# Layer 1 of a four-layer kernel: the experts' output bias fetched block by block, token counts by a scan, state-space products on two halves of the partitions

## What is computed

```python
# mixer
delta = softplus(x_inner @ W_dt + b_dt)
mean_delta = delta.mean(axis=-1)
a = exp(A[None, None, :] * mean_delta[..., None])        # 64 decays per token
bx = x_inner @ W_xp + b_xp                               # 64 inputs per token
state = a_t * state + bx_t                               # over 1024 tokens
s_sum = state.sum(axis=-1)
out = (s_sum[..., None] * x_inner * silu(res)) @ W_out + b_out + x * D
# feed-forward
shared = relu(normed @ sw1 + sb1) @ sw2 + sb2
comb = zeros(T, E).at[tokens, idx].add(w)                # w: the two weights of a token
h = relu(einsum('td,edh->teh', flat, ew1) + eb1)
eo = einsum('teh,eho->teo', h, ew2) + eb2                # eb2: the output bias, one row per expert
routed = einsum('teo,te->to', eo, comb)
return shared + routed
```

## Time and profile before

| | |
|---|---|
| time, median of 3 runs | 689.71 us (682.87 to 690.74) |
| profiled execution, span | 695.2 us |
| TensorE busy | 626.4 us (90%) |
| VectorE busy | 412.0 us (59%) |
| ScalarE busy | 366.7 us (53%) |
| GpSimd busy | 242.3 us (35%) |
| chain that ended last: TensorE | 59% of the span |
| DMA, mean of the span | 64 GB/s |

### The profile page before, as it was taken

The page is one execution under the profiler, slowest core; times in us unless marked ns, Lnnn a source line. Parts: engine busy times, 40 slices in busy tenths (PEclk is TensorE's granted clock), DMA queues, the critical chain, the costliest instruction groups (busy, mean ns, idle before and its releaser), DMA issues.

```text
span 695.2 us, 12273 instructions
## 1 busy us (share of the span) xinstructions
PE 626.4 (90%) x4105; PEld 404.3 (58%) x4108; DVE 412.0 (59%) x894; ACT 366.7 (53%) x849; POOL 242.3 (35%) x226
## 2 busy tenths in 40 slices
PE   8999999988987999888988889898888988799796
PEld 2885337974856667656656544345566665645353
DVE  6868754733345434956666478645868386455644
ACT  6346936325663443577478444362458468554342
POOL 2000660262373002757456323032138235523031
PEclk9999999989998999999999999999999999999999
DMA  8900212553443310000000210130000000040120
GB/s 302 361 20 0 95 58 86 155 163 123 135 128 102 98 62 28 24 9 2 16 17 1 68 58 0 38 101 1 16 1 2 1 1 1 8 117 0 48 91 16
DMA packets 29725, 44.48 MB, mean 64 GB/s; under 512 B 3928, under 2 KB 16064, under 8 KB 29152
## 3 DMA queue, kind: packets, MB, share of 16 engines
q1 hardware_dynamic: 26688, 36.48, 16.6%
q0 software_dynamic: 2976, 7.21, 3.4%
HBM read 34.37 MB, written 9.31 MB: 63 GB/s over the span
## 4 chain that ended last, share of the span: by engine, by line
PE 59%; DVE 18%; ACT 9%; issue 9%; POOL 3%; another core or an unknown queue 1%; DMA 1%; DVEq 0%; ACTq 0%; SPq 0%; POOLq 0%
PE bank L573 55%; ACT arena L1201 7%; DVE arena L2262 2%; DVE arena L2247 2%; DVE arena L2305 2%; POOL arena L2582 1%; DVE arena L2256 1%; DVE arena L2406 1%; DVE arena L2270 1%; PE bank L1067 1%; DVE bank L2298 1%; ACT rs L1201 1%; POOL arena L2590 1%; PE bank L948 1%; PE bank L762 1%
## 5 line engine op out<-in xcount | busy, mean ns | idle before, releaser
L1201 ACT ACTIVATE arena<-bank 128x512 f32<-128x512 f32 (+9 forms) x224 | 125.6, 565 | 102.8 <-PE bank L573 53.7
L1201 ACT ACTIVATE arena<-bank,arena 128x128 f32<-128x128 f32 (+1 forms) x244 | 87.8, 387 | 124.3 <-PE bank L573 61.5
L573 PE MATMUL bank<-arena,w 128*64 128x128 f32 (+2 forms) x528 | 143.2, 418 | 5.1 <-ACT arena L1201 5.0
L573 PE MATMUL bank<-arena 64*128 64x256 f32 (+8 forms) x832 | 108.8, 328 | 6.1 <-ACT arena L1201 6.1
L573 PE MATMUL bank<-xn_b,w 128*128 128x512 f32 (+1 forms) x192 | 91.4, 598 | 7.0 <-DVE arena L2406 3.8
L573 PEld LDWEIGHTS bank<-arena 64*128 64x128 f32 (+3 forms) x832 | 73.2, 169 | 33.1 <-ACT arena L1201 17.7
L573 PE MATMUL bank<-arena,work 128*128 128x128 f32 x624 | 85.7, 284 | 6.7 <-DVE arena L2152 2.6
L573 PEld LDWEIGHTS bank<-arena,work 128*128 128x128 f32 x624 | 78.2, 196 | 20.1 <-issue 16.0
L573 PEld LDWEIGHTS bank<-arena,w 128*128 128x128 f32 (+1 forms) x528 | 61.4, 163 | 39.1 <-issue 29.0
L573 PEld LDWEIGHTS bank<-xn_b,w 128*128 128x128 f32 (+1 forms) x192 | 34.5, 189 | 45.6 <-issue 28.6
L2490 POOL DMA_INDIRECT slots_in<-arena x32 | 33.8, 1057 | 77.2 <-ACT arena L1201 67.9
(11 more groups left out here) (222 smaller groups left out, 905.6 us busy)
## 6 DMA issues: line engine op xcount, KB each, us to landing
work<-in_ew SPq DMA_DIRECT2D x46, 256.0 KB
w<-kept SPq DMA_DIRECT2D x32, 128.0 KB, 3.0
work<-kept SPq DMA_DIRECT2D x32, 128.0 KB, 3.1
slots_in<-work SPq DMA_DIRECT2D x2, 1472.0 KB, 17.7
arena<-slots_in SPq DMA_DIRECT2D x10, 256.0 KB
slots_out<-arena POOLq DMA_DIRECT2D x10, 256.0 KB
w_ew<-in_ew SPq DMA_DIRECT2D x1, 2048.0 KB, 11.9
w<-in_p SPq DMA_DIRECT2D x1, 1840.5 KB, 9.8
```

The costliest lines, as they stand in the source:

```text
L573: return nc.tensor.matmul(o, lhsT, rhs, start=start, stop=stop, skip_group_check=True)
L1201: return nc.scalar.activation(o, i, f, bias=bias, scale=scale, **kw)
```

## The change

Four things change in layer 1, and nothing elsewhere.

1. **Output bias.** `cmb1`, its transposes, their copies and the product with `eb2` go. SP reads a second offset per block (`block_d`) and fetches that expert's 128 bias values into `bias2`, broadcast to 128 partitions (64 KB of writes), by a second DMA beside the weights'. `evicted` becomes a tensor_tensor add of PSUM and `bias2` in place of the copy.
2. **Token counts.** `cnt` is laid out expert by chunk, VectorE makes the counts of the chunks before by one scan of 72 elements (`before`), and TensorE needs two products for what took nine.
3. **State-space products.** `bx`, "md", the decays and the scan hold tokens 0 to 255 of a group on partitions 0 to 63 and 256 to 511 on 64 to 127. Products of 64 x 512 become two of 64 x 256 on the two halves. ScalarE reads [128 x 256] where it read [64 x 512]. The scan becomes two in sequence, with the last state of the one copied over to the other half (`seam`).
4. The weights' set "first" has one DMA more (`w1s` twice) and a wider constant (72 columns); "one" has one DMA less.

```diff
-                    mm(o, causal, cnt[:], stop=False)
-                    for c in range(1, 2 * C + 1):
-                        i = mm(o[:, c:], K["ones"], cnt[:, 0:2 * C + 1 - c], start=False, stop=c == 2 * C)
-                    i.then_inc(*step("cnt_p"))
+                    mm(o, ones, before[:], stop=False)
+                    mm(o[:, :, 0:2 * C], causal, cnt[:, :, 1:], start=False).then_inc(*step("cnt_p"))
...
+                    v.tensor_tensor_scan(before[:].rearrange("p e c -> p (e c)"), later, cnt[:].rearrange("p e c -> p (e c)"),
+                                         0.0, ALU.mult, ALU.add).then_inc(*step("before"))
...
+                    d = nc.values_load(block_d[0:1, n, k % NBLK:k % NBLK + 1], engines=[mybir.EngineType.SP], min_val=0,
+                                       max_val=(E1 - 1) * D)
+                    q, m = group(k), k % NBLK % SB
+                    if m == 0 and q >= 3:
+                        sp.wait_ge(*at_of(0, "rows_out", q - 3))
+                    sp.dma_start(bias2[:, q % 3, m], eb2.rearrange("(a e) d -> a (e d)", a=1)[:, bass.ds(d, D)].to_broadcast([P, D])).then_inc(
+                        bias2_in[q % 3], 16)
...
-                    pe.wait_ge(*at("cbt_s", g))
-                    mm(o[:], w_eb2, cbt1[:, gs(g)], start=False).then_inc(*step("sh", g))
-
-                def combined():
-                    pe.wait_ge(*at("cmb1"))
...
-                        i = mm(o[0:ST], W1["wxp"][:, j * ST:(j + 1) * ST], xi[:, j, gs(g)], start=j == 0, stop=j == 1)
+                        for h in range(2):
+                            i = mm(o[half_of(h), 0:GT // 2], W1["wxp"][:, j * ST:(j + 1) * ST], xi[:, j, hs(2 * g + h)],
+                                   start=j == 0, stop=j == 1)
...
-                    mm(o[0:ST], mean[:, 0:ST], dab[:, g]).then_inc(*step("md", g))
-                    yield
-                    o = fresh("quick", "ss", g)
+                    for h in range(2):
+                        i = mm(o[half_of(h), 0:GT // 2], mean[:, 0:ST], dab[:, g, hs(h)])
+                    i.then_inc(*step("md", g))
+                    yield
+                    o = fresh_pair("ss", g)
                     pe.wait_ge(*at("states", g))
-                    mm(o[:], ones[:], states[:, gs(g)]).then_inc(*step("ss", g))
+                    for h in range(2):
+                        i = mm(o[h][:, 0:GT // 2], ones[half_of(h)], states[half_of(h), hs(g)])
+                    i.then_inc(*step("ss", g))
...
+                    for h in range(2):
+                        start = 0.0
+                        if g or h:
+                            last = (2 * g + h) // 2 * GT // 2 - 1 if h == 0 else (g + 1) * GT // 2 - 1
+                            after()
+                            v.tensor_copy(seam[half_of(h), g:g + 1], states[half_of(1 - h), last:last + 1]).then_inc(*step())
+                            after()
+                            start = seam[half_of(h), g:g + 1]
+                        v.tensor_tensor_scan(states[half_of(h), hs(g)], decay[half_of(h), hs(g)], bx[half_of(h), hs(g)],
+                                             start, ALU.mult, ALU.add).then_inc(*step(*(("states", g) if h else ())))
...
-                        v.tensor_copy(rows_out[:, q % 2, 0:n], psum("eo", q)[:, 0:n * P].rearrange(
-                            "p (b d) -> p b d", d=P)).then_inc(*step("rows_out", q))
+                        dve.wait_ge(bias2_in[q % 3], 16 * sum(len(blocks_of(i)) for i in range(q % 3, q + 1, 3)))
+                        v.tensor_tensor(rows_out[:, q % 2, 0:n], psum("eo", q)[:, 0:n * P].rearrange(
+                            "p (b d) -> p b d", d=P), bias2[:, q % 3, 0:n], ALU.add).then_inc(*step("rows_out", q))
```

110 lines of the change are left out of this document (51 added, 59 removed), and 2 rows, old and new, of the table BESIDE.

## The result

| | before | after |
|---|---|---|
| time, median of 20 runs each | 685.48 us (682.22 to 691.64) | 680.93 us (676.01 to 684.64) |
| ratio after / before | | 0.9925, 95% interval 0.9904 to 0.9945 |
| profiled execution, span | 695.2 us | 676.3 us |

What follows compares the result with a forecast made beforehand. TensorE, busy 90% of the span, was taken to bound the kernel; -1.2 + 2.5 - 6.5 + 1.0 + 0.2 = -4.0 us gave 685.7 us from the median 689.7 (profiled 691.2), range for 8 in 10 676 to 695.

Steps and rivals of the forecast that it cites:

- the first case: Main forecast, the sum of the terms: 685.7 us from the median, own range 682 to 689, chance 0.50.
- rival 1: The clock does not fall and the gather absorbs nothing: -9.1 us, 680.6 us, chance 0.17.
- Ahead of the first block: TensorE sheds 7.2 us there but waits for expert rows; only the counts' 1.2 us is kept.
- Clock: TensorE's new wait for the first rows drops its clock to 0.50: 2.5 us lost, bounds 0 and 3.
- Beside the blocks: TensorE sheds 9.1 us beside the expert blocks; 2.6 us count as absorbed by the gather, so 6.5 us remain.
- SP: Added bias fetches in SP's queue cost 1.0 us in all, from dense runs of blocks; room on average.
- The wider set at the start: The wider "first" set of weights costs 0.2 us at the start.
- The rule weighed: Scans and GpSimd's products exclude one another; scans should run first, else "ss" of group 1 waits 1 to 2 us.
- 2: Rival: the halves run one after the other, or new waits eat as much: 688.6 to 690 us, chance 0.17.
- 3: Rival: SP's queue sets the pace of expert blocks: about 698 us, or 35 us more; chance 0.10.
- The stands between 140 and 218: TensorE's unexplained stands there; the forecast is wrong if they change length by more than 3 us each.
- the absorption: 2.6 us of TensorE's saving between the gather's start and its end at 215 counted as lost to GpSimd's queue.

Runs made afterwards that it cites:

- no_scan: Changed kernel with only the token counts undone (nine count products in place of a scan and two), chip 7: ratio 0.9985 to the kernel before.
- before_third: The kernel before, unchanged, profiled and timed a third time, on chip 10: 687.42 us, ratio 0.9999 to the kernel before.
- after_third: The changed kernel, unchanged, profiled and timed a third time, on chip 10: 680.24 us, ratio 0.9908 to the kernel before.
- halves_alone: The kernel before with only the state-space products and the scan put on two partition halves, chip 13: ratio 1.0054 to the kernel before.

## Why the prediction was right, point by point

The change came out within 1.1 us of the forecast (5.1 and 4.0 us). The time itself did not: 685.7 us were forecast from a median of three runs, 689.71, which is 685.48 over 20. The 680.93 us lie within the range for 8 in 10, but outside the 682 to 689 of the first case and near the 680.6 of rival 1. Much of what was to be seen in the profile was there: 0.5 us for the counts and the mixer's products from 67.06 (67.9 forecast; without the wait of 0.69 us in the earlier trace rows, but in five of the eight profiles with the scan TensorE waits 1.08 us for it), `bx` 1.0, "md" 0.65 with overlap, the clock at 0.50 behind the stand, SP's wait at 43.1 us (40). By the end of the blocks 4 to 5 us were to be gained; it is 7.4 on chip 10. The terms of the sum fared unequally.

- **Ahead of the first block, -1.2.** Right in size: 1.3 from no_scan and 1.4 between the two kernels on chip 10. The step to it was only half right. On chip 10 0.7 us is saved from `cnt` to `dest` and 1.3 by a shorter burst of scatters, which the prediction did not have; 0.6 is lost because `cnt` itself came later in that profile. In the first pair of profiles the loads of rows moved by 2.6 us (96.50 to 93.86), more than the 2 us it had set as a sign of being wrong; there the front alone begins about 0.8 us earlier. The stand is 4.45 us, not 6: TensorE would be through at 92.5, as worked out (92.7), but the rows come at 96.95 and not 98.7.
- **Clock, +2.5.** Mis-sized as a cost of the change. The fall alone costs 1.8 us, but the kernel before pays it too, in two profiles of three, and in before_third more than the change does. The step that failed was to read from the earlier trace rows, with its clock of 1.00, that before has no fall there. Net it is nothing or a gain: on chip 10, 3.1 of the 7.4 us arise between first block and counts, where the clock was at 0.50 longer before.
- **Beside the blocks, -6.5.** Right in kind, wrong in place. On chip 10 1.0 us comes through from the counts of batch 1 to the last store of batch 0, where TensorE has 2.4 us less to do, and 3.2 us behind the gather's landing ("ss" and the two bias products, worked out as 0.4 to 0.8 plus 2.1). Between the two 1.3 us are lost again. The 3.1 us before the counts hold "ss" of batch 0 and the clock, which cannot be told apart there.
- **SP, +1.0.** Too small. The prediction took SP's wait of 97.2 us as room on average, and allowed 0 to 3 us for dense runs of blocks. In the densest stretch that room is gone (a wait of 2.8 us in after_third from 118 to 158 us, 20.9 in before_third). No expert block waits for weights, but TensorE waits for rows whose loads stand behind the fetches, 1.4 us more on chip 10, and GpSimd's last store lands later, 0.9 us over all profiles. That is about 2.3 us.
- **The wider set at the start, +0.2.** Not tested apart.
- **The rule weighed.** The scans of the changed kernel did come ahead of GpSimd's products, except on chip 7. The price forecast for the other case was 1 to 2 us; in halves_alone it was 4.1 us at the first block (106.09 to 101.99, on two chips). The Trainium skill says in "SBUF — State Buffer", section "Who interferes with whom", that a VectorE instruction with two SBUF inputs and a GpSimd one that reads SBUF contend for the shared ports. The trace agrees: 6.00 us for a scan of 0.68.
- **Rivals.** 1, that the clock does not fall, fell: it falls. Its 680.6 us is near the time measured only because the median before came out lower; its saving of 9.1 us was not met. 2 fell: `bx` takes 1.0 us, half of 1.9, though halves without the other parts do lose. 3 fell for the layer as a whole, but in the dense stretch SP's queue does hold TensorE.
- **The stands between 140 and 218** I had called unexplained, and a reason to be wrong. Those at 140 to 163 go with the chip and not with the kernel. The one behind the gather goes with the kernel: it grew by 3.9 us on chip 10 (3.41 to 7.30), more than the 3 us named, because TensorE comes there earlier and the gather's landing does not keep up.

The terms that were off, the clock on one side and the absorption and SP on the other, had opposite signs. That the sum held better than its parts is luck.

## What to carry to other kernels

Split a stage into links by what sets each one, and count a saving only where the next thing waits for its engine: here TensorE's saving came through behind the gather, and of 2.4 us between counts and last store only 1.0. Look at a queue's room where its users are densest, and at everything that stands in it: SP had 43.1 us of waiting over the layer and hardly any from 118 to 158 us, and what came late was not what the added fetches bring but the rows behind them. A short instruction that can be held by another engine is as dear as what stands behind it in its queue; when something moves it by a microsecond, look at who overlaps it now. Take a second profile of the kernel before, on another chip if possible, ahead of reading single stands from the first.

## What the hardware showed

- One chip (7) ran the kernel before 11 us slower than the two others. Its last expert product ended 10.6 us later (274.13 beside 263.57), and the difference shows as stands of ScalarE, VectorE and TensorE while GpSimd issued indirect DMAs (ScalarE busy 3.5 to 5.5 us of 20, elsewhere 11 to 12).
- The scan was held although it began 0.52 us before GpSimd's product (92.43 and 92.95), and GpSimd's took its usual 4.93 us for four. The first to start was not the one that went on undisturbed, as far as the starts in the records can be trusted.
- TensorE's clock stood at 0.50 for some 8 us (102 to 110) in before_third, with TensorE busy in nearly all of it and only a stand of 0.73 us just before; in the first profile of the same kernel it stayed at 1.00 there.
- With 46 broadcast fetches of 64 KB in SP's queue, the gather that waits for another queue's store of 192 KB came 0.9 us later behind it (4.59 us in the mean of eight profiles, 3.71 in the mean of six without them), and loads of rows in SP's own queue came late enough for TensorE to stand 0.92 to 2.39 us (0.44 at most without them).
- GpSimd's burst of 16 indirect DMAs took 22.0 to 22.5 us in the six profiles with nine count products on TensorE ahead of it, 20.9 to 21.2 in the eight with the scan and two products. Nothing here shows why.
